# A four-layer graph attention stack: x loaded turned as well, the first loads in another order, and the softmax sums of both head halves in one PSUM region

## What is computed

```python
def _L0_gnn_ref(x, adj, ...):            # layer 0; layer 3 is the same but adds log(max(adj, 1e-8)) to the logits
    q, k, v = proj(Wq, bq), proj(Wk, bk), proj(Wv, bv)           # 8 heads of 32
    scores = einsum('bhqd,bhkd->bhqk', q, k) / sqrt(32)
    scores = where(adj + eye > 0, scores, -inf)
    out = einsum('bhqk,bhkd->bhqd', softmax(scores), v)
    h = x + (out @ Wo.T + bo)
    return layernorm(h) * gamma + beta
def _L1_gnn_ref(x, adjacency, ...):
    scores = einsum('bihd,bjhd->bhij', Q, K) / sqrt(32)
    scores = scores + (a[:, :, None] + c[:, None, :] + b_g + log(adjacency + 1e-9))   # a, c = x @ w_g[:D], x @ w_g[D:]
    return einsum('bhij,bjhd->bihd', softmax(scores), V) + x
def _L2_gnn_ref(feats, adj_mat, ...):    # one head: leaky_relu(q + k^T + mask), softmax, times feat_proj, plus feats
x = L3(L2(L1(L0(x, adj), adj), adj), adj)   # x, adj: (32, 256, 256) fp32
```

## Time and profile before

| | us |
|---|---|
| median of 3 runs | 1913.1 |
| lowest and highest | 1909.35, 1915.19 |
| the profiled execution's own time | 1908.63 |
| its span, first to last instruction | 1906.8 |
| PE busy (share of the span) | 1745.8 (92%) |
| PE weight loads | 1334.6 (70%) |
| DVE busy | 1550.6 (81%) |
| POOL busy | 1230.1 (65%) |
| ACT busy | 1216.3 (64%) |
| mean granted TensorE clock | 0.981 |

### The profile page before, as it was taken

One profiled execution on the slowest core, in us unless ns is written; L12 is line 12 of the kernel. 1 busy time (PEld: TensorE's weight loads), 2 busy tenths in 40 slices (PEclk: granted clock), 3 DMA queues, 4 the chain that ended last, 5 costly groups with the idle time before them and its releaser, 6 DMA issues.

```text
span 1906.8 us, 54647 instructions
## 1 busy us (share of the span) xinstructions
PE 1745.8 (92%) x23564; PEld 1334.6 (70%) x23564; DVE 1550.6 (81%) x2976; ACT 1216.3 (64%) x1894; POOL 1230.1 (65%) x743
## 2 busy tenths in 40 slices
PE   3899998899999999889999989888999999988996
PEld 2667776677777777577777767667777677766774
DVE  2889887777799988777889988777788998877775
ACT  1567665467777775456877767546777776654675
POOL 2534588368874377728895348754888445883688
PEclk9999999999999999999999999999999999999999
DMA  5110000100221001000111000010021100001001
GB/s 138 40 40 18 13 18 29 41 19 29 63 68 35 13 18 35 17 29 24 51 57 62 24 19 13 30 45 7 19 74 57 51 19 13 18 29 40 13 18 46
DMA packets 67731, 66.44 MB, mean 35 GB/s; under 512 B 6050, under 2 KB 67492, under 8 KB 67492
## 3 DMA queue, kind: packets, MB, share of 16 engines
q1 hardware_dynamic: 67492, 62.95, 11.1%
HBM read 54.54 MB, written 8.39 MB: 33 GB/s over the span
## 4 chain that ended last, share of the span: by engine, by line
PE 74%; DVE 19%; ACT 2%; issue 2%; SPq 1%; POOL 1%; DMA 0%; DVEq 0%; POOLq 0%; ACTq 0%
PE gx L589 22%; PE sc L694 16%; PE od L727 16%; PE gx L740 5%; PE gx L614 3%; PE sc L688 3%; DVE ring L969 3%; PE sc L700 3%; PE gx L776 3%; DVE negm L941 2%; DVE negm L944 2%; DVE qk L923 2%; PE gx L707 2%; DVE lg L1013 1%; DVE negm L957 1%
## 5 line engine op out<-in xcount | busy, mean ns | idle before, releaser
L574 POOL TENSOR_TENSOR ring<-ring,adj_c 128x1024 f32<-128x1024 f32 x256 | 610.4, 2409 | 170.0 <-ACT ring L837 113.0
L694 PE MATMUL sc<-qk 32*128 32x256 f32 x9216 | 417.4, 297 | 11.2 <-ACT m_rows L827 4.4
L694 PEld LDWEIGHTS sc<-qk 32*128 32x128 f32 x9216 | 326.0, 187 | 110.1 <-issue 64.3
L824 ACT ACTIVATE aside<-sc 128x1024 f32<-128x1024 f32 x192 | 196.6, 1024 | 236.1 <-PE sc L694 156.3
L941 DVE TENSOR_REDUCE negm<-sc 128x4 f32<-128x1024 f32 x192 | 234.1, 1219 | 86.2 <-PE sc L694 51.8
L839 ACT ACTIVATE ring<-sc 128x1024 f32<-128x1024 f32 x256 | 248.4, 1023 | 29.8 <-PE sc L700 29.3
L727 PE MATMUL od<-ring,vf 128*32 128x256 f32 x3072 | 243.4, 388 | 3.2 <-POOL ring L574 3.2
L553 POOL TENSOR_TENSOR xs<-xs,bo 128x512 f32<-128x512 f32 x96 | 128.0, 1333 | 182.0 <-DVE xt_lo L915 169.4
L727 PE MATMUL od<-ring,ones_r 128*32 128x256 f32 x3072 | 236.1, 379 | 0.0
L944 DVE TENSOR_REDUCE negm<-aside 128x4 f32<-128x1024 f32 x192 | 232.3, 1210 | 0.0
L579 POOL TENSOR_TENSOR xs<-xs,lr_g 128x512 f32<-128x512 f32 x64 | 86.9, 1357 | 169.8 <-ACT xs L846 169.8
(11 more groups left out here) (141 smaller groups left out, 4320.5 us busy)
## 6 DMA issues: line engine op xcount, KB each, us to landing
adj_c<-in_adj_t SPq DMA_DIRECT2D x96, 256.0 KB, 2.8
adj_r<-in_adj SPq DMA_DIRECT2D x64, 256.0 KB, 2.9
xs<-in_x SPq DMA_DIRECT2D x32, 256.0 KB, 3.1
out<-xs SPq DMA_DIRECT2D x32, 256.0 KB, 2.2
wo<-in_w_o SPq DMA_DIRECT2D x2, 256.0 KB
ring<-in_w_q SPq DMA_DIRECT2D x2, 256.0 KB, 6.5
ring<-in_w_k SPq DMA_DIRECT2D x2, 256.0 KB, 6.7
lr_g<-in_w_bg SPq DMA_DIRECT2D x2, 128.0 KB
```

What stands on the lines that cost most here:

```text
L574: pool.tensor_tensor(part, part, adj_c[i.mi % 3][:, t, :].unsqueeze(1).to_broadcast([P, G, N]), ALU.mult).then_inc(weighted, 1)
L694: mm = pe.matmul(sc[:, g, t * N:(t + 1) * N], buf[rows, a, c, t * P:(t + 1) * P], buf[rows, b, c, :], start=(n == 0 and not masked), stop= ...
L824: act.activation(aside[:], sc[:, 0:2, :], ACT.Copy).then_inc(set_aside, 1)
```

## The change

- **x turned.** The host hands over x also transposed (`x_t`). SP loads it for layer 0 into two new buffers `x_raw` (stage LT); stage T of layer 0 has no PE part any more, and ACT and DVE read `x_raw` in SBUF where they read `gx` in PSUM. The plain x is still loaded, for the residual. XB of layer 0 waits for that load instead of `xt_lo`.
- **First loads.** SP begins with turned x of graph 0, adjacency rows, the eight loads that `fold_biases` needs, and turned x of graph 1. ACT issues the weights of q, k, v of layer 0 and two bias columns. The other fifteen small loads and the seven later weights come behind plain x of graph 1. DVE makes `ident_r` before its first split.
- **The gate term.** The six matmuls "ca" of stage P in layer 1 are gone, with `cr_hi`, `cr_lo`, `row_sel` and L930. A new stage **O** takes column D+1 of `vf`: two small DVE instructions write its high and low part to `c_pad`, PE turns it with two 128x128 matmuls, ACT copies it to `c_rows`.
- **Sums.** The left factor of the sums is `halves[:, grp, :]`, 32 columns of which 16 are one and 16 zero, and both halves add up in the same region `od[1][:, 0:256]`; the values of both halves lie in `od[0]`. N becomes one stage per item: one transpose 128x256, one reciprocal 128x16, one transpose 128x512, one product 128x512. Chunk A.0 of the next item waits for all of it.
- **Tables.** Nearly all numbers of the plan tables are others.

```diff
-    "N": {DVE: [14.694, 16.472]},
...
+    "N": {DVE: [16.877]},
...
+    "O": {PE: [3.901], ACTE: [3.712], DVE: [2.701]},
...
+    "N": {DVE: [16.524]},
...
+    "LT": {SP: [-10.005]},
+    "LX": {SP: [-3.325]},
+    "LR": {SP: [-1.358]},
...
+            sp.dma_start(x_raw[0][:], x_t_all[items_l0[0].batch]).then_inc(xt_loaded[0], 16)
+            sp.dma_start(adj_r[0][:], adj_all[rows_of[0].batch]).then_inc(adjr_loaded[0], 16)
+            for dst, src in fold_plain:
+                sp.dma_start(dst, src).then_inc(w_fold, 16)
+            sp.dma_start(x_raw[1][:], x_t_all[items_l0[1].batch]).then_inc(xt_loaded[1], 16)
             for s, i, c in order[SP]:
-                if s == "LX":
+                if s == "LT" and i.i0 >= 2:
...
+                    if i.k == 1:
+                        for dst, src in plain:
+                            sp.dma_start(dst, src).then_inc(w_plain, 16)
+                        for n in range(3, len(WEIGHTS)):
                             load_weight(n)
...
+                elif s == "O":
+
+                    pe.wait_ge(c_pad_set, i.i1 + 1)
+                    pe.wait_ge(*gx_emptied("ca", i))
+                    for n in range(T):
+                        mm = pe.matmul(gx_of("ca", i)[:, n * P:(n + 1) * P], c_pad[i.i1 % 2][:, n, :], ident_r[:], start=True, stop=True)
+                    mm.then_inc(gx_sem("ca", i), 1)
...
-                    if t == 0 and i.mi:
-                        pe.wait_ge(o_set, C * (i.mi - 1) + grp + 1)
+                        pe.wait_ge(halves_set, C * C)
+                    if c == 0 and i.mi:
+                        pe.wait_ge(o_set, i.mi)
...
-                    for half in range(2):
+                    for den in range(2):
                         for g in range(G):
                             head = G * grp + g
-                            lhs = ones[:, 0:DH] if half else vf[i.mi % NVF][:, t, head * DH:(head + 1) * DH]
-                            mm = pe.matmul(od[grp][DH * g:DH * (g + 1), half * N:(half + 1) * N], lhs,
-                                           ring[:, ring_slot(i, c), g, :], start=(t == 0 and half == 0),
-                                           stop=(t == T - 1), skip_group_check=True)
-                    if t == T - 1:
+                            lhs = halves[:, grp, :] if den else vf[i.mi % NVF][:, t, head * DH:(head + 1) * DH]
+                            cols = slice(0, N) if den else slice(grp * N, (grp + 1) * N)
+                            mm = pe.matmul(od[den][DH * g:DH * (g + 1), cols], lhs, ring[:, ring_slot(i, c), g, :],
+                                           start=(c == 0), stop=(c == CH - 1 or (t == T - 1 and not den)), skip_group_check=True)
+                    if c == CH - 1:
                         mm.then_inc(av_done, 1)
                 elif s == "F":
...
+            for n in range(3):
+                if n == 1:
+                    for dst, src in first_plain:
+                        act.dma_start(dst, src).then_inc(w_first, 16)
+                name = WEIGHTS[n]
+                act.dma_start(staged[name][:, :, 0:D], w[name].rearrange("(c p) e -> p c e", p=P)).then_inc(w_raw[n], 16)
...
+                    if i.l == 0:
+                        act.wait_ge(xt_loaded[i.i0 % 2], 16 * (i.i0 // 2 + 1))
+                        if i.k >= 2:
+
+                            j = items[i.k - 2]
+                            what = "fp1" if j.l == GAT else "vb" if j.l == 1 else "v"
+                            act.wait_ge(gx_sem(what, j), gx_count(what, j))
...
+                    gate_c = vf[i.mi % NVF][:, :, D + 1:D + 2].to_broadcast([P, T, G])
+                    pad = c_pad[i.i1 % 2][:].rearrange("p t (g r) -> p t g r", g=G)
+                    dve.wait_ge(v_set, v_count(i))
+                    if i.i1 >= 2:
+                        dve.wait_ge(c_set, i.i1 - 1)
+                    dve.tensor_copy(pad[:, :, :, 0], gate_c).then_inc(c_hi_set, 1)
+                    dve.wait_ge(c_hi_set, i.i1 + 1)
+                    dve.tensor_tensor(pad[:, :, :, 1], gate_c, pad[:, :, :, 0].bitcast(F32), ALU.subtract).then_inc(c_pad_set, 1)
...
-                    grp = c
-                    dve.wait_ge(av_done, C * i.mi + grp + 1)
-
-                    dve.transpose(rden[grp][:], od[grp][:, N:2 * N]).then_inc(turned, 1)
-                    dve.wait_ge(turned, C * i.mi + grp + 1)
-                    dve.reciprocal(rden8[grp][:], rden[grp][:, 0:N:DH]).then_inc(inverted, 1)
-                    dve.wait_ge(inverted, C * i.mi + grp + 1)
-                    dve.transpose(rden[grp][:], rden8[grp][:].unsqueeze(2).to_broadcast([P, N // DH, DH])).then_inc(rden_set, 1)
-                    dve.wait_ge(rden_set, C * i.mi + grp + 1)
-                    dve.tensor_tensor(o_t[i.mi % 2][:, grp, :], od[grp][:, 0:N], rden[grp][:], ALU.mult).then_inc(o_set, 1)
+                    dve.wait_ge(av_done, i.mi + 1)
+
+                    dve.transpose(sums_t[:], od[1][:, 0:N]).then_inc(turned, 1)
+                    dve.wait_ge(turned, i.mi + 1)
+                    dve.reciprocal(rden8[:], sums_t[:, 0:N:DH // C]).then_inc(inverted, 1)
+                    dve.wait_ge(inverted, i.mi + 1)
+                    each = rden8[:].rearrange("p (b c) -> p c b", c=C).unsqueeze(3).to_broadcast([P, C, N // DH, DH])
+                    dve.transpose(rden[:].rearrange("p c (b r) -> p c b r", r=DH), each).then_inc(rden_set, 1)
+                    dve.wait_ge(rden_set, i.mi + 1)
+                    dve.tensor_tensor(o_t[i.mi % 2][:], od[0][:].rearrange("p (c n) -> p c n", c=C), rden[:], ALU.mult).then_inc(o_set, 1)
```

272 lines of the change are left out of this document (124 added, 148 removed).

## The result

The changed kernel takes 2061.7 us (median of four runs, 2060.57 to 2066.05), the kernel before 1911.9 beside it: a ratio of 1.079, 95% interval 1.076 to 1.081. The prediction, 2.2% faster, was wrong in sign and by 190 us. The profiled execution has a span of 2059.4 us.

A forecast was written before the change was run, and what follows sets the result against it. TensorE was taken as the bound, with VectorE close behind; start -16, stage T -16.5, gate term -16.6, sums +6 and +0.6, tables nothing: -42.5 from 1908.6 gives 1866.1, plus 4.5 to the median, 1870.6 us; range 1846 to 1892.

The forecast's parts named there:

- The tables: New stage order in all layers: TensorE's order nearly the old one, so taken at nothing (-24 to +10 us).
- its cause stays: End of layer 1: TensorE's 6.07 us wait before stage M, in each of four groups, stays because POOL's ring work slows stage U.
- the rule that speaks against the change: VectorE instructions with two SBUF inputs or fast copies exclude GpSimd's; stage O would pay up to two POOL instruction lengths.
- the slower rival: A.0 waiting for N cancels the gain; VectorE held by POOL in stage U, 1 us in 60 items: 1924 us, chance 0.04.
- The gate term: Layer 1: stage O's two matmuls, 0.28 us, replace six costing 0.80, over 32 items: -16.6 us.
- some 2.5 us of room: Stage O in layer 1: VectorE's part has this long before TensorE asks for it, so POOL's holds cost nothing.
- The sums: One stage N an item: A.0's wait costs +6 us (0 to +20) over 96 items, the last item's end +0.6.
- from none to 0.9 us: Slack for the single stage N before the next item's A.0 needs it, in layers 0, 1 and 3.
- Stage T: Layer 0: TensorE no longer turns x, 30 bursts at 0.55 us: -16.5 us.
- full price, since TensorE is the bound there: Layer 0: each burst taken from TensorE shortens the item by its whole length, 17.56 to about 17.0 us.
- The start: First loads reordered and x turned: first maximum at 27 to 32 us instead of 44.84, taken as -16 us (-12 to -20).
- from there both kernels do the same: After VectorE's first maximum both kernels run alike, so the start's gain of 16 us lasts to the end.

The follow-up runs named there:

- f_sums: The kernel before with only the sums of both head halves in one region, one stage N an item: 1949.4 us, 1.017 of before.
- g_turned: The kernel before with only x loaded turned and the first loads reordered, tables as before: 1914.4 us, 0.999 of before.
- a_tables: The changed kernel with the plan tables of the kernel before, its new stages added to them: 1951.2 us, 1.017 of before.
- h_gate: The kernel before with only stage O in place of the six matmuls for the gate term: 1999.4 us, 1.043 of before.
- q_a0_late: The kernel before with sums in one region and TensorE's A.0 (in layer 0 also A.1) moved behind ready work: 1927.5 us, 1.007 of before.

## Why the prediction was wrong

- **The tables (taken at nothing, -24 to +10; measured +110 to +117).** The largest error. The step was "its cause stays": the stand of 6 us before M in the earlier trace rows was read as four single events, since the order of TensorE's stages had hardly moved. What had moved was VectorE's order against POOL's. O, H and U of layer 1 came to stand beside 11.5 us of unbroken POOL work, and the stands became 24, 111.4 us in all. The mechanism was on the table, in the paragraph on the rule that speaks against the change, and in the slower rival ("VectorE held by POOL in stage U"), priced at 1 us an item in 60 items with a chance of 0.04. Cutting POOL's work in two showed it as the cause of 93 us. (That rival's own sum is off as well: 48 us of waits for N and 60 more on 1864.6 make some 1973, not 1924.)
- **The gate term (-16.6; measured alone +81.5).** The arithmetic on the bursts was right: O's two matmuls stand 0.34 us before the next burst (770.31 to 770.65) where 0.28 was forecast. The failed step is "some 2.5 us of room". I had counted what O needs, `c_pad`, and not the PSUM bank it writes to, which H empties.
- **The sums (+6 and +0.6; measured alone +31.5).** N's length was right, 2.15 forecast, 2.2 measured. The failed step is the slack "from none to 0.9 us", worked out as if VectorE started N at its turn after two maxima; in f_sums Q's parts and a layer norm stood between as well. The text named idle time before A.0 as the sign of this error, and it came: 46.7 us in place of 3.2 in f_sums, 57.2 in the changed kernel.
- **Stage T (-16.5; measured nothing).** The failed step is "full price, since TensorE is the bound there". The earlier trace rows had VectorE at 48 of 50 us. With T gone from TensorE, layer 0 of g_turned is 0.5 to 5.8 us a group longer, and VectorE busy for 138 of 145.5 us in the shortest. The relief of VectorE by the sums that was to make room was not in g_turned. In a_tables it is, with the old order, and there layer 0 takes 145.7, 144.6 and 144.6 us in groups two to four where the kernel before takes 144.8, 146.4 and 144.8; in the changed kernel it is 3.9 to 8.0 longer. So taking these instructions from TensorE shortened layer 0 in none of the three; which limit holds it there stays open. (A smaller slip: the row has 0.59 us a burst, the sum took 0.55.)
- **The start (-16).** The events came as forecast: projection at 6.9 (7 to 10), first maximum at 29.1 (27 to 32), first item 17 us earlier. In the changed kernel layer 0 of the first group still ends 14.8 us earlier, so the term itself came out near its size there; it was buried under the losses. Alone it did not reach the end time: x turned and the new loads gave 3.6 us, which is not clear of noise, the loads alone nothing. The failed step is "from there both kernels do the same": of the 12.5 us that g_turned has at the first maximum, 7.3 are left at the end of the first layer 0 and 2.4 at the end of the first group.
- **The chances.** 0.93 for faster rested on a sum whose losses were each bounded by the rows of an undisturbed order. In a program of queues in order, with a range of numbers exchanged, the losing side had no such bound.

## What to carry to other kernels

Before pricing a new order, lay VectorE's small SBUF-to-SBUF instructions beside GpSimd's list, not only TensorE's against TensorE's: a 0.2 us instruction with a long GpSimd instruction next to it costs the length of that one, and five in a row cost five; in an unbroken row of short GpSimd instructions one was even held for all of the row, 11.1 us. When reading idle time on a line of TensorE, do not add that of its weight loads to that of its matmuls: they pass together. Look at every group of a repeated pattern before multiplying the figure of one. For a new instruction name every resource it waits for, the bank it writes as well as the data it reads, and who empties that bank, behind what. If a wait moves onto an in-order queue, first try to put ready work ahead of the waiting instruction on *its* engine; moving its releaser forward delays what the releaser jumped over.

## What the runs showed of the hardware

A stand of TensorE can cost twice. Windows of h_gate: a score burst before the stand of 2.38 us shown above, and the same burst behind it (length, busy times, then the granted clock):

```profile
751.80:753.00 1.20, 1.20 (x40) 1.05 (x40) 0.84 (x2) 0.33 (x1) 1.20 (x1) 1.00 0.00 0
...
762.60:764.50 1.90, 1.90 (x35) 1.71 (x32) 0.00 (x0) 0.00 (x0) 1.90 (x3) 0.50 0.25 61
```

The granted clock was 0.50, the lower of the two levels (1.2 GHz of 2.4), and the burst took 1.98 us (762.55 to 764.53) where it takes 1.16 (751.78 to 752.94). Over 761.2 to 769.4 the clock was 0.59. It isn't so after every stand: of the 44 stands of over 2 us in the changed kernel 24 have a stretch at 0.50 that begins close to their end, 20 have none. In all, the clock was at 0.50 for 74 us of the kernel before, 197 of h_gate and 230 of the changed kernel. This goes with TensorE's busy time, which grew by 32.5 us in h_gate and 17.8 in the changed kernel, with fewer matmuls in both, and with layer 1's clock of 0.89 in the changed kernel, 0.95 before and 0.98 in q_a0_late.

And the cut of one GpSimd instruction into two made that engine 6% slower on the work (606.2 to 643.0 us) and the kernel 4.5% faster.
